# A rounding correction on GpSimd added behind two quantisation steps of a layer-norm, attention and BitLinear block

## The reference

```
xn  = (x - mean) / sqrt(var + 1e-5)                    # per token
att = softmax_causal(xn Wq (xn Wk)^T / 32) (xn Wv)
s   = 127 / max(max|xn|, 1e-5);   qx = round(xn * s)    # per token, 8 bit
h   = silu(depthwise_conv3(qx/s @ ternary(w1)^T) + cb)  # 4096 hidden
s2  = 127 / max(max|h|, 1e-5);    qh = round(h * s2)
out = x + att + qh/s2 @ ternary(w2)^T
```

## Time and profile before

| | us |
|---|---|
| median of two runs | 5953.05 (5937.48 to 5968.62) |
| profiled execution | 5959.59 |
| its span on the slowest core | 5957.8 |
| spans of the eight cores | 5893.0 to 5957.8 |

### The profile page before, as it was taken

How to read it: one execution, slowest core, us unless ns; L and a number is a source line. 1 busy time by engine, 2 the same in 40 slices (tenths; PEclk the granted TensorE clock), 3 DMA queues, 4 the chain that set the end, 5 groups by cost and what they waited for, 6 DMA issues and landing times.

```text
span 5957.8 us, 41297 instructions; the slowest of 8 cores (5893.0 to 5957.8 us)
## 1 busy us (share of the span) xinstructions
PE 2407.1 (40%) x11579; PEld 1247.8 (21%) x11579; DVE 2766.1 (46%) x3581; ACT 1011.6 (17%) x1291; POOL 173.8 (3%) x296
## 2 busy tenths in 40 slices
PE   1115886666674111332332432432432432432432
PEld 0112332233331001211211211211221221221221
DVE  5552001222112556656556456456456455555555
ACT  3332221111111000021111111111112112112112
POOL 0000000000000100000000000000000000000000
PEclk9999886777776555666666676766666766766766
DMA  6662123000001333100000000000000000000000
GB/s 57 53 53 59 48 80 106 26 18 15 11 13 54 123 134 124 37 22 9 14 22 9 14 23 9 14 23 9 14 22 9 14 22 9 18 19 9 23 14 7
DMA packets 100201, 202.06 MB, mean 34 GB/s; under 512 B 43056, under 2 KB 59536, under 8 KB 95888
## 3 DMA queue, kind: packets, MB, share of 16 engines
q0 software_dynamic: 36928, 149.06, 10.3%
q1 hardware_dynamic: 63056, 50.37, 3.5%
HBM read 149.04 MB, written 50.35 MB: 33 GB/s over the span
## 4 chain that ended last, share of the span: by engine, by line
DVE 40%; PE 30%; ACT 13%; issue 9%; DMA 6%; DVEq 1%; ACTq 0%; POOL 0%; POOLq 0%; SPq 0%
PE psM L946 8%; PE psPV L580 5%; PE pj L358 4%; DVE scr L1069 4%; PE psS L503 4%; ACT ihb L1218 3%; DVE h L1036 3%; DVE ihb L1225 3%; DVE scr L993 3%; DVE scr L1017 3%; DVE scr L1003 3%; DVE scr L1010 3%; DVE scr L1027 3%; DVE h L1190 3%; ACT psuQ L1209 3%
## 5 line engine op out<-in xcount | busy, mean ns | idle before, releaser
L946 PE MATMUL psM<-ixw,w1qT 128*128 128x260 bf16 x4096 | 616.3, 324 | 517.9 <-DVE h L963 334.8
L1159 PE MATMUL psM<-w2qT,ihb 128*128 128x512 bf16 x2048 | 596.7, 457 | 455.1 <-DVE ihb L1225 455.1
L946 PEld LDWEIGHTS psM<-ixw,w1qT 128*128 128x128 bf16 x4096 | 467.4, 115 | 670.0 <-issue 537.9
L1101 PE MATMUL psX<-identf,scr 128*128 128x128 f32 x32 | 14.3, 447 | 1205.9 <-DVE scr L1093 1205.9
L963 DVE TENSOR_TENSOR h<-psM,sxb 128x260 f32<-128x260 f32 x512 | 219.5, 429 | 513.6 <-PE psM L946 482.3
L1049 ACT ACTIVATE h<-h 128x4096 f32<-128x4096 f32 x32 | 116.6, 3645 | 1922.9 <-DVE h L1036 1922.9
L1225 DVE SCALAR_TENSOR_TENSOR ihb<-ihb,ubf 128x1024 bf16<-128x1024 bf16 x128 | 156.9, 1226 | 571.1 <-ACT ihb L1218 571.1
L1159 PEld LDWEIGHTS psM<-w2qT,ihb 128*128 128x128 bf16 x2048 | 222.9, 113 | 822.6 <-issue 688.7
L1203 ACT ACTIVATE ubf<-h 128x1024 bf16<-128x1024 f32 x128 | 136.0, 1063 | 875.9 <-DVE h L1190 875.9
L358 PE MATMUL pj<-xnT,wb 128*128 128x512 bf16 x1024 | 252.7, 416 | 48.3 <-DVE wb L345 48.3
L1101 PEld LDWEIGHTS psX<-identf,scr 128*128 128x128 f32 x32 | 5.8, 182 | 1217.5 <-issue 1217.5
(11 more groups left out here) (129 smaller groups left out, 3387.0 us busy)
## 6 DMA issues: line engine op xcount, KB each, us to landing
scr<-w POOLq DMA_DIRECT2D x64, 512.0 KB, 3.5
scr<-w POOLq DMA_DIRECT2D x32, 1024.0 KB, 5.4
xin<-x POOLq DMA_DIRECT2D x32, 512.0 KB, 10.6
xres<-x POOLq DMA_DIRECT2D x32, 512.0 KB, 3.6
out<-xres SPq DMA_DIRECT2D x32, 512.0 KB, 2.6
ixw<-ixT_s POOLq DMA_DIRECT2D x16, 516.0 KB, 6.0
ixT_s<-ixstg SPq DMA_DIRECT2D x32, 256.0 KB, 12.9
qT_s<-spst SPq DMA_DIRECT2D x64, 128.0 KB, 1.9
```

The lines of the kernel that those rows point to most:

```text
L946: P.emit("tensor", (lambda h2_, di_, ps_, rhs_: lambda t: t.matmul(bass.AP(ps_[:].tensor, 0, [[260, 128], [130, 2], [1, 130]]), w1qT[:, H ...
L1159: P.emit("tensor", (lambda: lambda t: t.matmul(psM2[:, 512 * hf_:512 * (hf_ + 1)], ihb[:, 1024 * r_ + 128 * hq_:1024 * r_ + 128 * (hq_ + 1 ...
```

## The change

After each of the two quantisation steps a correction is added to the integer tile. Two constants are new, 1.5*2^52 (`CBIG`) and 1.5*2^31 (`CMID`). With v the scaled value before rounding, the added instructions form ((v + CBIG) - CBIG) - ((v + CMID) - CMID) and add it to the integer tile. They all run on GpSimd, and each handles 128 x 1024 elements and waits for the one in front of it. No instruction is removed.

- Normalisation, five per tile: scale `csc` into `sqs` (waits for `xq_guard` and the reduction of `sqs`), the CBIG pass into `csc` (waits for `xnb`), the CMID pass in place in `sqs`, the difference into `csc`, and `ixb += csc` (waits for L276). The transposes of `ixb` wait for the fifth. The next tile's writes of `sqs` and `csc` wait for the fourth and fifth.
- `stage2`, four per quarter: the CMID pass of `h2` into a free part of `scr16` (waits for L1190), the CBIG pass in place in `h2` (waits for `arel`), the difference in `h2`, and `ihb += h2` (waits for L1225). The 16 matmuls wait for the fourth, and `h2rel` holds it.

```diff
@@ normalisation, behind L276 @@
                     bbP_guard = P.now("v")
-                ix_done = P.now("v")
+                    P.emit("gpsimd", lambda g: g.tensor_scalar(
+                        out=sqs[:], in0=csc[:], scalar1=colD[:], scalar2=None,
+                        op0=ALU.mult),
+                        waits=[xq_guard, sqs_free, P.now("g")], inc="g")
+                    P.emit("gpsimd", lambda g: g.tensor_scalar(
+                        out=csc[:], in0=sqs[:], scalar1=CBIG, scalar2=CBIG,
+                        op0=ALU.add, op1=ALU.subtract),
+                        waits=[xnb_done, P.now("g")], inc="g")
+                    P.emit("gpsimd", lambda g: g.tensor_scalar(
+                        out=sqs[:], in0=sqs[:], scalar1=CMID, scalar2=CMID,
+                        op0=ALU.add, op1=ALU.subtract),
+                        waits=[P.now("g")], inc="g")
+                    P.emit("gpsimd", lambda g: g.tensor_tensor(
+                        out=csc[:], in0=csc[:], in1=sqs[:], op=ALU.subtract),
+                        waits=[P.now("g")], inc="g")
+                    sqs_gguard = P.now("g")
+                    P.emit("gpsimd", lambda g: g.tensor_tensor(
+                        out=ixb[:], in0=ixb[:], in1=csc[:], op=ALU.add),
+                        waits=[bbP_guard, P.now("g")], inc="g")
+                    csc_gguard = P.now("g")
+                ix_done = P.now("g") if safe else P.now("v")
@@ stage2, behind L1225, per quarter @@
-                    h2rel[par][qq] = (h, arel)
-                ih_q = P.now("v")
+                    gvq = bass.AP(scr16[:].tensor, 2564,
+                                  [[HC * 128, 128], [128, 8], [1, 128]])
+                    P.emit("gpsimd", ... tensor_scalar(
+                        out=o_, in0=hq_, scalar1=CMID, scalar2=CMID,
+                        op0=ALU.add, op1=ALU.subtract))(h2qA, gvq),
+                        waits=[pm, sw2_ready, P.now("g")], inc="g")
+                    P.emit("gpsimd", ... tensor_scalar(
+                        out=hq_, in0=hq_, scalar1=CBIG, scalar2=CBIG,
+                        op0=ALU.add, op1=ALU.subtract))(h2qA),
+                        waits=[arel, P.now("g")], inc="g")
+                    P.emit("gpsimd", ... tensor_tensor(
+                        out=hq_, in0=hq_, in1=o_, op=ALU.subtract))(h2qA, gvq),
+                        waits=[P.now("g")], inc="g")
+                    ihap = bass.AP(ihb[:].tensor, 1024 * ring,
+                                   [[2048, 128], [128, 8], [1, 128]])
+                    P.emit("gpsimd", ... tensor_tensor(
+                        out=ia_, in0=ia_, in1=hq_, op=ALU.add))(h2qA, ihap),
+                        waits=[ubf_guard[ring], P.now("g")], inc="g")
+                    h2rel[par][qq] = (h, P.now("g"))
+                ih_q = P.now("g") if safe else P.now("v")
```

More of the change, by code:

```diff
@@ L21 @@
 LADDER = [64.0, 32.0, 16.0, 8.0, 4.0, 2.0, 1.0, 0.5]
+CBIG = float(1.5 * 2.0 ** 52)
+CMID = float(1.5 * 2.0 ** 31)
 ENGS = ("tensor", "vector", "scalar", "gpsimd", "sync")
@@ L189, in build_nc @@
             xnb_tguard = None
+            csc_gguard = None
+            sqs_gguard = None
             xin_guard = [None, None, None]
@@ L212, in build_nc @@
                     out=csc[:], in0=xa_[:], scalar1=colA[:], scalar2=None, op0=ALU.subtract))(xa),
-                    waits=[P.now("v")] + ([xq_guard] if xq_guard else []), inc="v")
+                    waits=[P.now("v")] + ([xq_guard] if xq_guard else [])
+                          + ([csc_gguard] if csc_gguard else []), inc="v")
                 cdone = P.now("v")
@@ L217, in build_nc @@
                                                         bias=0.0, scale=1.0),
-                       waits=[cdone], inc="s")
+                       waits=[cdone] + ([sqs_gguard] if sqs_gguard else []), inc="s")
                 P.emit("vector", lambda v: v.reduce_sum(out=colB[:], in_=sqs[:], axis=AX.X),
                        waits=[P.now("s")], inc="v")
+                sqs_free = P.now("v")
                 P.emit("scalar", lambda s: s.activation(out=colB[:], in_=colB[:], func=ACT.Sqrt,
@@ L1231, in stage2 @@
                     ubf_guard[ring] = P.now("v")
-                    h2rel[par][qq] = (h, arel)
-                ih_q = P.now("v")
+                    gvq = bass.AP(scr16[:].tensor, 2564,
+                                  [[HC * 128, 128], [128, 8], [1, 128]])
+                    P.emit("gpsimd", (lambda hq_, o_: lambda g: g.tensor_scalar(
+                        out=o_, in0=hq_, scalar1=CMID, scalar2=CMID,
+                        op0=ALU.add, op1=ALU.subtract))(h2qA, gvq),
+                        waits=[pm, sw2_ready, P.now("g")], inc="g")
+                    P.emit("gpsimd", (lambda hq_: lambda g: g.tensor_scalar(
+                        out=hq_, in0=hq_, scalar1=CBIG, scalar2=CBIG,
+                        op0=ALU.add, op1=ALU.subtract))(h2qA),
+                        waits=[arel, P.now("g")], inc="g")
+                    P.emit("gpsimd", (lambda hq_, o_: lambda g: g.tensor_tensor(
+                        out=hq_, in0=hq_, in1=o_, op=ALU.subtract))(h2qA, gvq),
+                        waits=[P.now("g")], inc="g")
+                    ihap = bass.AP(ihb[:].tensor, 1024 * ring,
+                                   [[2048, 128], [128, 8], [1, 128]])
+                    P.emit("gpsimd", (lambda hq_, ia_: lambda g: g.tensor_tensor(
+                        out=ia_, in0=ia_, in1=hq_, op=ALU.add))(h2qA, ihap),
+                        waits=[ubf_guard[ring], P.now("g")], inc="g")
+                    h2rel[par][qq] = (h, P.now("g"))
+                ih_q = P.now("g") if safe else P.now("v")
                 if dbg == f"ih{pr}_{par}_{qq}":
```

## The result

The changed kernel takes 7268.14 us (median of 11 runs, 7241.03 to 7305.95) against 5935.53 us for the kernel before on the same chips (10 runs): a ratio of 1.2239, 95% interval 1.2206 to 1.2271. The direction was forecast, the size was not: 1333 us more, where the forecast was 621 and the range ended at 6900.

What follows compares the result with a forecast made beforehand. The prediction took chains of dependent work, not a full engine, as the bound. It added 272 us (normalisation) and 349 us (stage two), 621 us, to the profiled 5959.6 for 6581, or 6575 as the median; range 6230 to 6900.

Steps and rivals of the forecast that it cites:

- The bound and the chains: Whole kernel: no engine is full, VectorE busiest at 46%; chains of dependent work set the time.
- S: Both stages: a one-input GpSimd pass over 1024 columns takes 1.05 us, from the memsets.
- The upper bound: Both stages: a GpSimd reading and writing in turn needs 2.0 us for one-input passes, 2.96 for two-input ones.
- rival 2: Both stages: slow GpSimd passes, 2.0 us one-input and 2.96 two-input, in turn with VectorE; about 7120 us, chance 10%.
- T: Both stages: a two-input GpSimd pass takes 2.2 us, two reads in turn and a tenth for the write.
- In turn or not: Both stages: added GpSimd passes and VectorE operations with two SBUF inputs take turns; a quarter takes 9.3 us instead of 7.0.
- The exposed load: Normalisation: the next tile's load, queued behind the fifth correction, lands 3.8 us after issue; VectorE waits about 2.5 us.
- rival 3: Normalisation: each input load takes 10.6 us to land, 218 us more, 6793 us; chance 6%.
- Rival 4: Stage two: longer pauses may keep each tile's last TensorE burst slow, 85 us more, 6660 us; chance 12%.
- Rival 5: Both stages: GpSimd passes faster than its memset and beside VectorE; at 0.5 us each 96 us, 6050; chance 3%.
- rival 1: Both stages: GpSimd and VectorE overlap freely; 6274 us, or 6150 with two-input passes at 1.05 us; chance 17%.

Runs made afterwards that it cites:

- e1: The changed kernel with only the five normalisation corrections, the four per FFN quarter taken out: 6375.38 us, ratio 1.0758 to the kernel before.
- e2: The changed kernel with only the four corrections per FFN quarter, the five of the normalisation taken out: 6815.35 us, ratio 1.1494 to the kernel before.
- e4: The changed kernel with its two-constant passes cut to one operation (adding 0.0), the first of each FFN quarter to a plain copy: 6844.64 us, ratio 1.1543.
- e5: The changed kernel with input loads issued three tiles ahead, in front of the corrections in GpSimd's queue: 7217.02 us, ratio 1.2099.
- e7: The kernel before plus three two-input GpSimd passes per FFN quarter on scratch columns, for which nothing waits: 6165.52 us, ratio 1.0344.
- e8: The kernel before plus two one-input, two-constant GpSimd passes per FFN quarter on scratch columns, for which nothing waits: 6001.08 us, ratio 1.0079.
- e10: The changed kernel with its one-input passes moved to VectorE and the two-input ones left on GpSimd: 6443.44 us, ratio 1.0800.

## Why the prediction failed: one price

**The bound and the chains: right.** The chains of dependent work set the time, the added passes lie on them, and the losses of the stages add up (e1, e2).

**S, the one-input pass: the step that failed.** "One pass over 1024 columns is then 1.05 us", from the slope of two memsets. A memset writes a number that it has; nothing is computed per column. The copy in e4 does run at that rate (1.04), but one operation costs 1.7 us more and the second 0.9. Passes of S's kind were taken at 1.05 and measured 2.84, 3.63 and 3.63 in the normalisation: 6.95 us a tile more, 222 us. In stage two there are two a quarter, 2 x 2.58 x 128 = 661 us. The upper bound failed too: "would need two passes for a one-input operation (2.0 us)" bounds the movement of data and not the work on it, so even the dear rival 2 had S at 2.0, too cheap by 1.6. That it came near the result (7120) is luck: its T was 0.6 to 1.0 too dear, and it counted the turns in full.

**T, the two-input pass: right.** 2.2 assumed, 2.34 and 2.13 measured in the normalisation and 2.00 and 2.13 in stage two, undisturbed: 33 us less in all.

**In turn or not: right for T, wrong for S.** The forecast let VectorE and every pass take turns. Over the four quarters of a tile its turns and gaps come to 9.8 us (38.8, less the start at 1.45, 1.55 of waiting for |h| and 26.0 of passes). In the changed kernel GpSimd's chain lasts 52.2 us on average over the 32 tiles, and its 16 passes would take 45.6 undisturbed. That leaves 6.6, since VectorE's operations mostly slipped under the one-input passes: 3.2 x 32 = 102 us in the other direction. What is held can be seen in the groups of the first and the last pass of a quarter, undisturbed 3.63 and 2.13:

```profile
L1260 POOL TENSOR_SCALAR scr<-h 128x1024 f32<-128x1024 f32 x128 | 507.2, 3962 | 2351.8 <-DVE h L1216 2336.2 <-POOL ihb L1273 14.7 <-ACT psuQ L1235 1.0
...
L1273 POOL TENSOR_TENSOR ihb<-ihb,h 128x1024 bf16<-128x1024 bf16 x128 | 314.5, 2457 | 18.9 <-POOL h L1268 0.9
```

In the normalisation L282 took no turn at all, some 1 us a tile or 34 us less.

**The balance.** 222 + 661 us for S, less 33 for T, less 34 and 102 for the turns, less 50 because the first pass of a tile's stage two now hides the wait for |h| (1.55 us in the forecast's chain), plus 56 at the tail, which is further down: 720 us. Less the 30 between the stages and at their edges that is 690 of the 697 us by which the profile exceeds the forecast. 7 us stay without a name.

**The sum with the measured prices.** Normalisation: GpSimd's chain starts at 10.3, needs 14.6 and four gaps of 0.15, and the load 3.7: 29.2, measured 29.0. For stage two such a sum proves less, because its quarter of 12.9 us is itself the measured one: start 1.5, four quarters, 0.25 to the matmul, 53.4 against 53.5. It shows only that nothing else stands on the way to the last burst.

**The exposed load: right.** About 2.5 us of waiting in 30 tiles, as listed among the signs; the load lands in 3.7 us, so rival 3 (10.6) is out. Taking it away gives 2.2 us a tile back (e5).

**TensorE's clock: a term that the forecast put at nothing.** Rival 4 had it at 85 us, and some 50 of them came. A table of the four bursts of one tile in the changed kernel, TensorE busy and granted clock:

```profile
5028.60:5034.80 6.20, 6.05 (x16) 0.59 0.00 0
...
5068.40:5073.50 5.10, 4.94 (x16) 0.73 0.00 0
```

The two bursts between ran at 0.63 and 0.58. Before, one or more of a tile's bursts ran at 1.00, that is 2.4 GHz; here all lie between the two levels, and the last takes 4.94 us instead of 3.61. Averaged over the 32 tiles, the last burst starts 53.98 us after the first multiply instead of 28.24 and lasts 5.56 us instead of 3.98. The longer burst is 1.6 us a tile, 51 us, and with some 0.2 us behind it this makes the 56 us of the tail.

**Rival 5, quick passes:** out. The two-input part of rival 1 is out too (e7).

## What to carry to other kernels

An engine that is idle is not a cheap one: before work is handed to it, find a row with the same form of instruction, and where there is none, treat the price as open upwards, since a memset or a copy bounds the movement of data but not the arithmetic. Here the corrections cost 1333 us on the idle GpSimd, 752 on the busiest engine and 476 shared out by form. Ask as well what else stands in the queue of the engine that gets the work: the loads that stood behind other work were worth 68 us of the normalisation in the changed kernel and some 220 us in the one before.

## What the runs showed of the hardware

- GpSimd on 128 x 1024 float32: copy 1.04 us at least, one scalar operation 2.77 (2.84 with a per-partition scale), two 3.63, one tile minus itself 1.89, two tiles 2.0 to 2.34. On VectorE the pass with two constants took 0.69 and the two-input one 1.23.
- A one-input GpSimd pass keeps VectorE's two-input operations off for the first 0.9 us of its 3.6 (128 of 128 operations in e8); a two-input one for its whole length (e7).
- Not only two-input operations of VectorE wait. In e10 the one-input pass of VectorE that takes 0.69 us alone takes 2.23 beside GpSimd's two-input pass:

```profile
4547.04 0.69 DVE L1253 TENSOR_SCALAR scr<-h 128x1024 f32<-128x1024 f32 x1 [0.31 <-DVE h L1216]
...
4553.65 1.22 DVE L1216 TENSOR_TENSOR h<-h,scr 128x1024 f32<-128x1024 f32 x1
4553.75 3.12 POOL L1275 TENSOR_TENSOR ihb<-ihb,h 128x1024 bf16<-128x1024 bf16 x1 [1.29 <-DVE ihb L1262]
...
4555.18 2.23 DVE L1253 TENSOR_SCALAR scr<-h 128x1024 f32<-128x1024 f32 x1 [0.31 <-DVE h L1216]
```

The GpSimd pass at 4553.75 is held by VectorE's multiply until 4554.9 and ends at 4556.87; the VectorE pass of 4555.18 ends at 4557.41, behind it.
- The eight cores differ more between the two changed stages than the change does. From the last normalisation reduction to the first FFN matmul the slowest cores took 1962.5 us before and 1950.5 after, as if this stretch had become faster. On cores 0 to 5 it took 1902 to 1921 us before and 1912 to 1919 after (core 0: 1908.1 and 1915.6), somewhat longer, as the rest of the last tile's corrections would have it. The longer normalisation did not raise TensorE's clock either: the granted clock of the first 630 us of the projections was 0.81 before, 0.84 after, and 0.86 in e2, whose normalisation is as short as before.
